# Reordered first attention, q's lower halves on GpSimd, and separate first products in the gated network

## The chip, the cores and the metric

One core of one Trainium2 chip runs the whole kernel. The metric is the device time of one execution in microseconds. Three runs of the kernel before gave 2217.47, 2220.65 and 2222.77 us; the median is 2220.65 us.

## What is computed

The input is 32 samples of 256 tokens, each of width 128, in float32. Two layers follow each other. Each layer is an attention and a feed-forward part, and each part has the form x = x + gate * part(layernorm(x) * (1 + scale) + shift), with gate, scale and shift made per sample from a conditioning vector.

- First attention: RMS norm, then 16 query heads and 8 key and value heads of width 64 (two query heads share one key head). Queries and keys are normalised per head, and the scores go through a soft clamp before the causal softmax:

```
sim = tanh(q @ k.T / 50) * 50 * 64**-0.5
attn = softmax(where(causal, sim, -inf));  out = (attn @ v) @ Wout
```

- First feed-forward part: a router with 16 experts and a shared expert.
- Second attention: 16 heads of width 8 with low-rank projections and rotary parts.
- Second feed-forward part, the gated network, hidden width 512:

```
h = silu((x @ w1) * s1) * ((x @ w2) * s2)
h = gelu((h @ h1) * t1);  h = gelu((h @ h2) * t2);  return (h @ w3) * s3
```

## The kernel before

The kernel keeps all of x in SBUF and runs four stages one after another, each a block with its own instruction list for every engine. The order of the work on each engine is written out by hand: a loop over n, in whose body the pieces of several samples stand in a fixed order, and semaphores join the engines. An engine works its list strictly in order, so a piece that waits holds everything behind it.

**First attention** (function `attention0`, lines 250 to 909). The loop goes over 32 samples. In iteration n the scores of sample n run, while sample n+1 has its queries and keys normalised and turned, sample n+2 is projected, and sample n-1 is gathered and written back to x. The names are:

- The 16 heads are four groups g of four heads. `pe_scores` (L407) writes the scores of a group into the one score buffer `pS` of three PSUM banks; ScalarE's `act_softmax` takes them by tanh (L793) into `th` and by the exponential (L797) into `pr`, one instruction each of 1536 elements per partition. GpSimd's `gp_mask` (L861, two instructions) zeroes the part above the diagonal, and `pe_weighted_values` (L422, L423) multiplies by the values, two heads p at a time. VectorE's `dve_outputs` (L633, L637) divides by the sum, and GpSimd's `gp_sum` (L869) adds the two heads that share a value head into `as`.
- `pe_heads_back` (L444) transposes `as` in two halves t, `act_take_heads` (L803) copies each half into `at`, and `pe_out_project` (L458) multiplies `at` by the output weights. `act_gate` (L787), `pe_out_back` (L464) and `dve_add` (L113) bring it into x.
- Queries and keys are used as a float16 pair, an upper half (the value rounded to float16) and a lower half (what is left). `dve_norm` (L628) scales them, `act_hi` (L775) writes the upper halves and `dve_lo` (L642) the lower ones, by subtraction; u = 0 is k (512 elements), u = 1 is q (1024 elements), and t is the half of the tokens. `pe_turn_k` (L375) and `pe_turn_q` (L391) transpose them into PSUM banks `pW`; `act_take_k` (L781) and `dve_take_q` (L650) copy them out. Two DMAs of SP then make a swapped copy of the keys.
- `pe_project_qk` (L363) makes six products m of 512 columns in the banks `pW`. The products 3 and 4 wait for `dve_take_q` of another sample, product 5 waits for `dve_add`.

In ScalarE's order of iteration n stand tanh and exponential of group 2, then `act_take_heads(n-1, 1)`. On TensorE the matching stretch is: weighted values 3, `pe_out_project(n-1)`, both `pe_turn_k(n+1)`, scores 3, weighted values 4, `pe_turn_q(n+1, 0)`, weighted values 5, `pe_turn_q(n+1, 1)`, `pe_out_back`, products 3, 4 and 5. GpSimd's order is: mask 0, sums 6 and 7 of n-1, mask 1, sums 0 and 1, mask 2, sums 2 and 3, mask 3, sums 4 and 5. Sum 0 of a sample waits until TensorE has transposed the `as` of the sample before, both halves.

**Gated network** (function `mlp`, lines 1718 to 2044). It goes over 16 runs of 512 tokens. All activations are float16 pairs again. For each of four hidden tiles j, `pe_first` (L1783) makes two products, `pA` (for w1) and `pB` (for w2), two matmuls each, and signals once after both. Then `act_tanh` (L1982) reads `pA`, `dve_gated` makes `gf` (L1884) from tanh and `pA` and `uf` (L1888) from `gf` and `pB`, `act_hi` (L1989) and `dve_gated_low` (L1899) split `uf`. `pe_second` and `pe_third` (both L1796) are the two hidden layers in four waves w of 2, 6, 10 and 14 matmuls. Wave w needs the split tile w. `act_gelu` (L2001) takes a finished tile, `dve_parts` (L1878, L1880) splits it. `pe_out` (L1812) is the last product, `act_gate` (L1975) scales it, `pe_back` (L1820) turns it back, and `dve_add` (L1904) adds it to x. `dve_front` (L103), `pe_front` (L1773), `act_modulate` (L1967) and `dve_split_h` (L1878, L1880) prepare the input of a run. The transposes of front and back share one PSUM bank, `pX`; so `pe_back(n-1)` has to wait until `act_modulate(n+1)` has read the bank.

The order on VectorE in iteration n is: low 3 (n), split of the input (n+1), parts 0, 1, 2 of the second layer (n), gated 0 (n+1), parts 3, gated 1, low 0, front (n+2), parts 0 and 1 of the third layer, low 1, parts 2, gated 2, `dve_add(n-1)`, parts 3, low 2, gated 3.

## Time and profile before

| what | value |
|---|---|
| median of three runs | 2220.65 us |
| the profiled execution's own time | 2222.54 us |
| its span | 2220.8 us |
| TensorE busy | 2074.2 us, 93% |
| VectorE busy | 1709.8 us, 77% |
| ScalarE busy | 1444.2 us, 65% |
| GpSimd busy | 521.8 us, 23% |
| mean granted clock of TensorE | 0.978 of full speed |

First attention takes the span from its start to about 1050 us, the gated network from about 1850 us to the end. Busy times are shares of the whole span. Matmuls are pipelined and their recorded ends are modelled, so the start of the next group is a better mark than the end of the last.

### The profile page before, as it was taken

The numbers are of one execution on the slowest core, as the hardware profiler recorded it, in microseconds if no ns is written. First come the engines' busy times: TensorE is split into PE (matmuls) and PEld (weight loads), VectorE is DVE, ScalarE is ACT, GpSimd is POOL, SyncE is SP. The second block draws the span as 40 slices with busy tenths as digits, with TensorE's granted clock in tenths as the row PEclk, the third lists the DMA queues.
The fourth block names the chain that finished last, engine by engine and source line by source line (L and its number), as shares of the span: only waits on it lengthen the run. The fifth ranks groups of instructions, "written<-read, shape, count | busy, mean of one in ns | idle before, by whom it ended". The sixth has DMA issues, their size and how long they took to land. (4 is left out here: it accounts for less than half of the span.)

```text
span 2220.8 us, 40446 instructions
## 1 busy us (share of the span) xinstructions
PE 2074.2 (93%) x14885; PEld 1370.3 (62%) x14885; DVE 1709.8 (77%) x4079; ACT 1444.2 (65%) x1931; POOL 521.8 (23%) x798
## 2 busy tenths in 40 slices
PE   3899999999999999998899999799999996999998
PEld 1577777777777777776444444477777773444443
DVE  3988898888898888983666666577777766888887
ACT  1777777777777777773566666466666663555554
POOL 1243333333333333333000000133333330000000
PEclk9999999999999999997899999899999997999999
DMA  5000000000000000000100000000000000000000
GB/s 160 20 20 20 14 16 21 20 20 20 11 20 20 20 20 20 11 20 20 43 1 1 1 1 0 1 2 2 2 2 2 2 2 1 10 11 15 10 15 19
DMA packets 32836, 35.31 MB, mean 16 GB/s; under 512 B 6865, under 2 KB 26497, under 8 KB 32641
## 3 DMA queue, kind: packets, MB, share of 16 engines
q1 hardware_dynamic: 32640, 32.73, 5.6%
q8 instruction: 120, 1.97, 0.4%
q14 instruction: 76, 0.61, 0.1%
HBM read 11.75 MB, written 4.19 MB: 7 GB/s over the span
## 5 line engine op out<-in xcount | busy, mean ns | idle before, releaser
L861 POOL TENSOR_SCALAR_AFFINE_SELECT pr<-pr 128x512 f32<-128x512 f32 x256 | 208.7, 838 | 534.3 <-ACT pr L797 534.2
L422 PE MATMUL a_pO<-va,pr 128*128 128x66 f32 x2048 | 304.7, 272 | 2.0 <-POOL pr L861 2.0
L422 PEld LDWEIGHTS a_pO<-va,pr 128*128 128x128 f32 x2048 | 273.6, 193 | 19.0 <-issue 14.8
L1620 ACT ACTIVATE c_pr<-c_pS 128x1536 f32<-128x1536 f32 x128 | 186.0, 1453 | 119.2 <-PE c_pS L1432 119.2
L1675 POOL TENSOR_SCALAR_AFFINE_SELECT c_pr<-c_pr 128x512 f32<-128x512 f32 x256 | 158.3, 643 | 265.2 <-DVE c_pr L1540 265.2
L765 ACT ACTIVATE sq<-a_pW 128x512 f32<-128x512 f32 x192 | 114.4, 597 | 143.4 <-PE a_pW L363 140.8
L793 ACT ACTIVATE th<-a_pS 128x1536 f32<-128x1536 f32 x128 | 186.3, 1455 | 30.6 <-PE a_pS L407 30.1
L423 PE MATMUL a_pO<-va,pr 128*128 128x66 f32 x1024 | 199.0, 276 | 0.0
L797 ACT ACTIVATE pr<-th 128x1536 f32<-128x1536 f32 x128 | 189.9, 1484 | 4.1
L407 PE MATMUL a_pS<-qs,k 128*128 128x512 f16 (+1 forms) x1024 | 187.8, 326 | 0.7 <-DVE qs L650 0.7
L1540 DVE TENSOR_SCALAR c_pr<-c_pr 128x1536 f32<-128x1536 f32 x128 | 122.6, 958 | 78.4 <-ACT c_pr L1620 78.4
L869 POOL TENSOR_TENSOR as<-on 128x128 f32<-128x128 f32 x256 | 144.9, 578 | 115.2 <-PE a_pW L444 95.8
L1013 PE MATMUL b_pU<-b_hT,b_uT 128*128 128x512 f32 x320 | 168.9, 611 | 0.0
L1031 PE MATMUL b_pD<-b_a,b_dT 128*128 128x512 f32 x320 | 163.0, 592 | 0.0
L1179 DVE TENSOR_TENSOR b_a<-b_q,b_pC 128x512 f32<-128x512 f32 x128 | 87.7, 685 | 96.3 <-ACT b_q L1263 96.2
L407 PEld LDWEIGHTS a_pS<-qs,k 128*128 128x128 f16 x1024 | 98.9, 98 | 99.8 <-issue 35.3
L1250 ACT ACTIVATE b_r<-b_pU 128x512 f32<-128x512 f32 x160 | 95.4, 596 | 95.6 <-PE b_pU L1013 95.6
L423 PEld LDWEIGHTS a_pO<-va,pr 128*128 128x128 f32 x1024 | 156.4, 193 | 0.0
L581 DVE TENSOR_TENSOR qg<-a_pW,a_gam 128x512 f32<-128x512 f32 x192 | 130.7, 682 | 8.2 <-ACT sq L765 8.1
L633 DVE RECIPROCAL rl<-a_pO 128x4 f32<-128x4 f32 x256 | 44.7, 175 | 112.2 <-PE a_pO L423 112.2
L363 PE MATMUL a_pW<-a_wq,hT 128*128 128x512 f32 x256 | 129.2, 628 | 0.7 <-DVE qs L650 0.7
L1796 PE MATMUL d_pH<-d_a,d_h1T 128*128 128x512 f16 x512 | 122.7, 383 | 3.6 <-DVE d_a L1899 3.6
(259 smaller groups left out, 4439.3 us busy)
## 6 DMA issues: line engine op xcount, KB each, us to landing
k<-k SPq DMA_DIRECT2D x64, 256.0 KB, 3.6
x<-in_L_attn_tokens_dram SPq DMA_DIRECT2D x8, 512.0 KB, 7.0
out_dram<-x SPq DMA_DIRECT2D x16, 256.0 KB, 2.3
d_h<-in_L_ffn_h_w_dram SPq DMA_DIRECT2D x2, 1024.0 KB, 7.3
wmod<-in_L_wmod_dram SPq DMA_DIRECT2D x2, 384.0 KB, 3.6
d_w<-in_L_ffn_w_w_dram SPq DMA_DIRECT2D x3, 256.0 KB, 3.1
a_wq<-in_L_attn_Wq_dram SPq DMA_DIRECT2D x1, 512.0 KB, 6.6
a_wkv<-in_L_attn_Wkv_dram SPq DMA_DIRECT2D x1, 512.0 KB, 6.9
```

The costliest lines, as they stand in the source:

```text
L407: last = pe.matmul(out, kk[:, h // G2, keys * P:(keys + 1) * P], qs[k][:, h:h + G2, keys * P:N], start=first, stop=not first)
L422: pe.matmul(out, w[:, hh * N + t * P:hh * N + (t + 1) * P], v[:, 0, p, :], start=True, stop=t == 0)
L423: last = pe.matmul(out, w[:, HPG * N + hh * P:HPG * N + (hh + 1) * P], v[:, 1, p, :], start=False, stop=True)
L581: dve.tensor_tensor(qg[n % 2][:, t, cols], pW[BANK_OF[m]][:, :], gam[:, cols], ALU.mult).then_inc(s_qg, 1)
L793: act.activation(th[:, :], pS[:, :], ACT.Tanh, scale=1.0 / SOFTCLAMP).then_inc(s_th, 1)
L797: act.activation(pr[g % 2][:, :], th[:, :], ACT.Exp, scale=SOFTCLAMP * DH ** (-0.5)).then_inc(s_pr, 1)
L861: last = gp.affine_select(out=part, in_=part, compare_op=ALU.is_ge, fill=0.0, base=0, pattern=[[0, HPG], [1, P]], channel_multiplier=-1)
L869: gp.tensor_tensor(as_[:, :, p * DH:(p + 1) * DH], o[:, :, 0, :], o[:, :, 1, :], ALU.add).then_inc(s_as, 1)
L1013: pe.matmul(pU[u % 2][:, :], uT[:, t * P:(t + 1) * P], hT[n % 2][:, :], start=True, stop=True).then_inc(s_up, 1)
L1031: pe.matmul(pD[:, :], dT[:, t * D:(t + 1) * D], a[(IT * n + u) % 4][:, :], start=u == 0, stop=u == IT - 1).then_inc(s_dn, 1)
L1620: act.activation(pr[g][:, :, :], pS[:, :, 0:N + P], ACT.Exp, scale=float(1.0 / np.sqrt(np.float32(DQ)))).then_inc(s_ex, 1)
L1675: last = gp.affine_select(out=part, in_=part, compare_op=ALU.is_ge, fill=0.0, base=0, pattern=[[0, HPG], [1, P]], channel_multiplier=-1)
```

## The change

First attention:
- `act_softmax` is split into `act_tanh` and `act_exp`; they follow each other as before, but in group 2 `act_take_heads(n-1, 1)` now stands between them.
- On TensorE `pe_turn_k(n+1, 0)` moves ahead of `pe_out_project(n-1)`, and `pe_turn_q(n+1, 1)` moves ahead of weighted values 5, right behind `pe_turn_q(n+1, 0)`. On VectorE `dve_take_q(n+1, 1)` moves ahead of outputs 5.
- The two lower halves of q (L642, u = 1) leave VectorE for GpSimd, with a semaphore of their own, `s_ql`. On GpSimd the first stands behind sums 0 and 1 and ahead of mask 2, the second behind sum 2 and ahead of sum 3.

Gated network:
- `pe_first` makes one of the two products per call, each with its own signal (`s_in` for `pA`, `s_ib` for `pB`). Tanh and `gf` need only `pA`, `uf` waits for `s_ib`. `gf` has two buffers.
- On TensorE the halves of the first products are spread between waves of the hidden layers, and `pe_front(n+2)` and the output product stand at the end of the iteration, front ahead of first product 3.
- `act_modulate(n+2)` now stands between tanh 3 and the gate at the end of ScalarE's iteration, where `act_modulate(n+1)` stood at the start of it.
- `dve_add(n-1)` moves from behind gated 2 to ahead of gated 0.

```diff
...
         def pe_turn_k(pe, n, t):
-            pe.wait_ge(s_lo, 4 * n + t + 1)
+            pe.wait_ge(s_lo, 2 * n + t + 1)
             if n >= 2:
...
             if j == 0:
-                pe.wait_ge(s_lo, 4 * n + 2 + t + 1)
+                pe.wait_ge(s_ql, 2 * n + t + 1)
...
                     pe_weighted_values(pe, n, 3)
+                if 0 <= n + 1 < B:
+                    pe_turn_k(pe, n + 1, 0)
                 if 0 <= n - 1 < B:
                     pe_out_project(pe, n - 1)
                 if 0 <= n + 1 < B:
-                    pe_turn_k(pe, n + 1, 0)
                     pe_turn_k(pe, n + 1, 1)
                 if 0 <= n < B:
                     pe_scores(pe, n, 3)
                     pe_weighted_values(pe, n, 4)
                 if 0 <= n + 1 < B:
                     pe_turn_q(pe, n + 1, 0)
+                    pe_turn_q(pe, n + 1, 1)
                 if 0 <= n < B:
                     pe_weighted_values(pe, n, 5)
-                if 0 <= n + 1 < B:
-                    pe_turn_q(pe, n + 1, 1)
                 if 0 <= n - 1 < B:
                     pe_out_back(pe, n - 1)
                 if 0 <= n + 2 < B:
...
-                dve.wait_ge(s_lo, 4 * n - 4)
+                dve.wait_ge(s_lo, 2 * n - 2)
+                dve.wait_ge(s_ql, 2 * n - 2)
...
-        def dve_lo(dve, n, u, t):
-            dve.wait_ge(s_hi, 4 * n + 2 * u + t + 1)
+        def lower(eng, n, u, t, done):
+            eng.wait_ge(s_hi, 4 * n + 2 * u + t + 1)
             to, x = ((kp, qg[n % 2][:, t, QW:]), (qp, qg[n % 2][:, t, 0:QW]))[u]
-            dve.tensor_tensor(to[:, t, :, DH:2 * DH], x.rearrange('p (h d) -> p h d', d=DH), to[:, t, :, 0:DH], ALU.subtract).then_inc(s_lo, 1)
+            eng.tensor_tensor(to[:, t, :, DH:2 * DH], x.rearrange('p (h d) -> p h d', d=DH), to[:, t, :, 0:DH], ALU.subtract).then_inc(done, 1)
...
                     dve_sums(dve, n + 2, 0)
-                if 0 <= n + 1 < B:
-                    dve_lo(dve, n + 1, 1, 0)
                 if 0 <= n < B:
                     dve_outputs(dve, n, 2)
                 if 0 <= n + 2 < B:
                     dve_ln(dve, n + 2, 2)
...
-                if 0 <= n + 1 < B:
-                    dve_lo(dve, n + 1, 1, 1)
...
                     dve_take_q(dve, n + 1, 0)
+                    dve_take_q(dve, n + 1, 1)
                 if 0 <= n < B:
                     dve_outputs(dve, n, 5)
-                if 0 <= n + 1 < B:
-                    dve_take_q(dve, n + 1, 1)
                 if 0 <= n + 3 < B:
...
-        def act_softmax(act, n, g):
+        def act_tanh(act, n, g):
             act.wait_ge(s_sc, 4 * n + g + 1)
             if n or g:
                 act.wait_ge(s_pr, 4 * n + g)
             act.activation(th[:, :], pS[:, :], ACT.Tanh, scale=1.0 / SOFTCLAMP).then_inc(s_th, 1)
+
+        def act_exp(act, n, g):
             act.wait_ge(s_th, 4 * n + g + 1)
             if n or g >= 2:
                 act.wait_ge(s_pv, 8 * n + 2 * g - 2)
...
                 if 0 <= n < B:
-                    act_softmax(act, n, 2)
+                    act_tanh(act, n, 2)
                 if 0 <= n - 1 < B:
                     act_take_heads(act, n - 1, 1)
+                if 0 <= n < B:
+                    act_exp(act, n, 2)
                 if 0 <= n + 1 < B:
                     act_hi(act, n + 1, 1, 1)
...
+                if 0 <= n + 1 < B:
+                    lower(gp, n + 1, 1, 0, s_ql)
                 if 0 <= n < B:
                     gp_mask(gp, n, 2)
                     gp_sum(gp, n, 2)
+                if 0 <= n + 1 < B:
+                    lower(gp, n + 1, 1, 1, s_ql)
+                if 0 <= n < B:
                     gp_sum(gp, n, 3)
                 if 0 <= n < B:
                     gp_mask(gp, n, 3)
...
-        def pe_first(pe, n, j):
+        def pe_first(pe, n, j, half):
             if j == 0:
                 pe.wait_ge(s_hx, n + 1)
-            for out, w, taken in ((pA, w1T, s_gf), (pB, w2T, s_uf)):
-                if n or j:
-                    pe.wait_ge(taken, 4 * n + j)
-                for part in range(2):
-                    last = pe.matmul(out[:, :], w[:, j * P:(j + 1) * P], hx[:, part, :], start=part == 0, stop=part == 1)
-            last.then_inc(s_in, 1)
+            out, w, taken, done = ((pA, w1T, s_gf, s_in), (pB, w2T, s_uf, s_ib))[half]
+            if n or j:
+                pe.wait_ge(taken, 4 * n + j)
+            for part in range(2):
+                last = pe.matmul(out[:, :], w[:, j * P:(j + 1) * P], hx[:, part, :], start=part == 0, stop=part == 1)
+            last.then_inc(done, 1)
 
...
-            for n in range(-2, RUNS + 1):
-                if 0 <= n - 1 < RUNS:
-                    for i in range(HT):
-                        pe_out(pe, n - 1, i)
-                if 0 <= n + 1 < RUNS:
-                    pe_front(pe, n + 1)
+            for n in range(-3, RUNS + 1):
...
-                    pe_first(pe, n + 1, 0)
+                    pe_first(pe, n + 1, 0, 0)
                 if 0 <= n < RUNS:
                     pe_third(pe, n, 0)
+                if 0 <= n + 1 < RUNS:
+                    pe_first(pe, n + 1, 0, 1)
+                if 0 <= n < RUNS:
                     pe_third(pe, n, 1)
                 if 0 <= n + 1 < RUNS:
-                    pe_first(pe, n + 1, 1)
+                    pe_first(pe, n + 1, 1, 0)
+                    pe_first(pe, n + 1, 1, 1)
                 if 0 <= n < RUNS:
                     pe_third(pe, n, 2)
                     pe_third(pe, n, 3)
                 if 0 <= n + 1 < RUNS:
-                    pe_first(pe, n + 1, 2)
+                    pe_first(pe, n + 1, 2, 0)
                     pe_second(pe, n + 1, 0)
+                    pe_first(pe, n + 1, 2, 1)
                     pe_second(pe, n + 1, 1)
-                    pe_first(pe, n + 1, 3)
+                if 0 <= n + 2 < RUNS:
+                    pe_front(pe, n + 2)
+                if 0 <= n + 1 < RUNS:
+                    pe_first(pe, n + 1, 3, 0)
+                if 0 <= n < RUNS:
+                    pe_out(pe, n, 0)
+                if 0 <= n + 1 < RUNS:
+                    pe_first(pe, n + 1, 3, 1)
+                if 0 <= n < RUNS:
+                    for i in range(1, HT):
+                        pe_out(pe, n, i)
 
         def dve_front(dve, n):
             if n >= 1:
...
-                dve.wait_ge(s_in, 4 * n)
+                dve.wait_ge(s_ib, 4 * n)
             split(dve, n, hx[:, 0, :], hx[:, 1, :], hf[:, :], s_hh, n + 1, s_hx)
...
-            dve.scalar_tensor_tensor(gf[:, :], th[:, :], 1.0, pA[:, :], ALU.add, ALU.mult).then_inc(s_gf, 1)
+            dve.scalar_tensor_tensor(gf[j % 2][:, :], th[:, :], 1.0, pA[:, :], ALU.add, ALU.mult).then_inc(s_gf, 1)
             dve.wait_ge(s_gf, 4 * n + j + 1)
             if n or j >= 2:
                 dve.wait_ge(s_a1, 4 * n + j - 1)
-            dve.scalar_tensor_tensor(uf[j % 2][:, :], gf[:, :], s12[:, j:j + 1], pB[:, :], ALU.mult, ALU.mult).then_inc(s_uf, 1)
+            dve.wait_ge(s_ib, 4 * n + j + 1)
+            dve.scalar_tensor_tensor(uf[j % 2][:, :], gf[j % 2][:, :], s12[:, j:j + 1], pB[:, :], ALU.mult, ALU.mult).then_inc(s_uf, 1)
 
         def dve_parts(dve, n, layer, o):
...
+                if 0 <= n - 1 < RUNS:
+                    dve_add(dve, n - 1)
                 if 0 <= n + 1 < RUNS:
                     dve_gated(dve, n + 1, 0)
                 if 0 <= n < RUNS:
...
-                if 0 <= n - 1 < RUNS:
-                    dve_add(dve, n - 1)
                 if 0 <= n < RUNS:
                     dve_third(dve, n, 3)
...
                     act_hi(act, n, 3)
-                if 0 <= n + 1 < RUNS:
-                    act_modulate(act, n + 1)
-                if 0 <= n < RUNS:
                     act_second(act, n, 0)
                     act_second(act, n, 1)
                     act_second(act, n, 2)
...
+                if 0 <= n + 2 < RUNS:
+                    act_modulate(act, n + 2)
                 if 0 <= n < RUNS:
                     act_gate(act, n)
 

```

## Rows read from the trace of the kernel before

**Rows 1.** Busy time by stretch: the steady parts of first attention and network

```profile
core 0: us, PE busy (x) PEld busy (x) DVE busy (x) ACT busy (x) POOL busy (x), PEclk, DMA share, GB/s
...
135.00:1000.00 865.00, 833.36 (x6127) 633.28 (x6125) 757.97 (x1632) 663.06 (x766) 314.87 (x458) 1.00 0.07 18
...
1915.00:2200.00 285.00, 271.76 (x1260) 119.20 (x1259) 249.48 (x454) 152.41 (x263) 0.00 (x0) 1.00 0.05 14
```

**Rows 2.** Waits of all engines, 135 to 1000 us: us in total, times, longest

```profile
PE a_pW L458 <- ACT at L803: 28.8, 29, 2.5
```

**Rows 3.** Timeline, one sample of first attention: start, us, engine, line, operation

```profile
421.25 0.87 POOL L869 TENSOR_TENSOR as<-on 128x128 f32<-128x128 f32 x2 [3.11 <-PE a_pW L444]
...
421.30 1.48 ACT L797 ACTIVATE pr<-th 128x1536 f32<-128x1536 f32 x1
...
422.00 0.39 PE L423 MATMUL a_pO<-va,pr 128*128 128x66 f32 x2
...
422.69 0.58 ACT L803 ACTIVATE at<-a_pW 128x512 f32<-128x512 f32 x1
...
423.32 1.99 PE L458 MATMUL a_pW<-at,a_wo 128*128 128x256 f32 x8 [0.94 <-ACT at L803]
...
425.16 1.06 PE L375 MATMUL a_pW<-id,kp 128*128 128x128 f16 x16
...
426.05 1.46 PE L407 MATMUL a_pS<-qs,k 128*128 128x512 f16 x8
...
427.35 0.56 PE L422 MATMUL a_pO<-va,pr 128*128 128x66 f32 x4
...
428.41 0.39 PE L423 MATMUL a_pO<-va,pr 128*128 128x66 f32 x2
...
428.64 0.61 PE L391 MATMUL a_pW<-id,qp 128*128 128x128 f16 x8
```

**Rows 4.** Timeline of first attention: four matmuls and the next group, twice

```profile
409.13 1.94 PE L363 MATMUL a_pW<-a_wq,hT 128*128 128x512 f32 x4
...
410.90 1.46 PE L407 MATMUL a_pS<-qs,k 128*128 128x512 f16 x8
...
431.10 1.95 PE L363 MATMUL a_pW<-a_wq,hT 128*128 128x512 f32 x4
...
433.15 1.12 PE L363 MATMUL a_pW<-a_wkv,hT 128*128 128x512 f32 x2
```

**Rows 5.** Timelines: GpSimd's instructions, one of VectorE beside them

```profile
35.80 2.48 POOL L883 TENSOR_TENSOR a_gam<-a_gam,a_gk 128x512 f32<-128x512 f32 x2
35.88 1.20 DVE L91 TENSOR_TENSOR ln_tmp<-rs 128x4 f32<-128x4 f32 x1
...
431.04 1.23 POOL L861 TENSOR_SCALAR_AFFINE_SELECT pr<-pr 128x512 f32<-128x512 f32 x2 [4.71 <-ACT pr L797]
```

**Rows 6.** Page, part 5: GpSimd's sums

```profile
L869 POOL TENSOR_TENSOR as<-on 128x128 f32<-128x128 f32 x256 | 144.9, 578 | 115.2 <-PE a_pW L444 95.8
```

**Rows 7.** Timeline of the gated network: first tanh, then one run

```profile
1860.95 0.69 ACT L1982 ACTIVATE d_th<-d_pA,d_s1h 128x512 f32<-128x512 f32 x1 [3.17 <-PE d_pB L1783]
...
2051.20 0.43 DVE L1878 CAST d_a<-d_ge 128x512 f16<-128x512 f32 x1 [0.78 <-ACT d_ge L2001]
...
2054.66 0.69 DVE L1884 SCALAR_TENSOR_TENSOR d_gf<-d_th,d_pA 128x512 f32<-128x512 f32 x1 [0.17 <-ACT d_th L1982]
...
2057.55 0.69 DVE L1884 SCALAR_TENSOR_TENSOR d_gf<-d_th,d_pA 128x512 f32<-128x512 f32 x1 [0.36 <-ACT d_th L1982]
...
2070.15 0.69 DVE L1899 TENSOR_TENSOR d_a<-d_uf,d_a 128x512 f16<-128x512 f32 x1 [0.70 <-ACT d_a L1989]
...
2071.17 0.63 PE L1820 MATMUL d_pX<-id,d_og 128*128 128x128 f32 x4 [0.38 <-ACT d_hf L1967]
...
2071.64 3.19 PE L1796 MATMUL d_pH<-d_a,d_h1T 128*128 128x512 f16 x14
...
2072.99 0.43 DVE L1878 CAST d_a<-d_ge 128x512 f16<-128x512 f32 x1 [0.78 <-ACT d_ge L2001]
```

More of the change, by code:

```diff
@@ L289, in attention0 @@
         s_xn, s_xT, s_hT, s_hsq, s_ms, s_msv = (sem(x) for x in ('xn', 'xT', 'hT', 'hsq', 'ms', 'msv'))
-        s_qk, s_sq, s_qg, s_ss, s_f, s_qn, s_hi, s_lo = (
-            sem(x) for x in ('qk', 'sq', 'qg', 'ss', 'f', 'qn', 'hi', 'lo'))
+        s_qk, s_sq, s_qg, s_ss, s_f, s_qn, s_hi, s_lo, s_ql = (
+            sem(x) for x in ('qk', 'sq', 'qg', 'ss', 'f', 'qn', 'hi', 'lo', 'ql'))
         s_qt, s_qs, s_kt, s_ks = (sem(x) for x in ('qt', 'qs', 'kt', 'ks'))
@@ L704, in _ @@
                 if 0 <= n + 1 < B:
-                    dve_lo(dve, n + 1, 0, 0)
+                    lower(dve, n + 1, 0, 0, s_lo)
                 if 0 <= n + 2 < B:
@@ L710, in _ @@
                 if 0 <= n + 1 < B:
-                    dve_lo(dve, n + 1, 0, 1)
+                    lower(dve, n + 1, 0, 1, s_lo)
                 if 0 <= n + 2 < B:
                     dve_sums(dve, n + 2, 0)
-                if 0 <= n + 1 < B:
-                    dve_lo(dve, n + 1, 1, 0)
                 if 0 <= n < B:
@@ L821, in _ @@
                 if 0 <= n < B:
-                    act_softmax(act, n, 0)
+                    act_tanh(act, n, 0)
+                    act_exp(act, n, 0)
                 if 0 <= n + 2 < B:
@@ L826, in _ @@
                 if 0 <= n < B:
-                    act_softmax(act, n, 1)
+                    act_tanh(act, n, 1)
+                    act_exp(act, n, 1)
                 if 0 <= n + 1 < B:
@@ L850, in _ @@
                 if 0 <= n < B:
-                    act_softmax(act, n, 3)
+                    act_tanh(act, n, 3)
+                    act_exp(act, n, 3)
                 if 0 <= n + 2 < B:
@@ L1741, in mlp @@
         hx = sb('hx', [D, 2, W], F16)
-        th, gf, uf = (sb('th', [P, W]), sb('gf', [P, W]), [sb(f'uf{k}', [P, W]) for k in range(2)])
+        th, gf, uf = (sb('th', [P, W]), [sb(f'gf{k}', [P, W]) for k in range(2)], [sb(f'uf{k}', [P, W]) for k in range(2)])
         a1, a2, a3 = (sb(x, [P, HT, 2, W], F16) for x in ('a1', 'a2', 'a3'))
@@ L1754, in mlp @@
         s_xn, s_xT, s_hf, s_hh, s_hx = (sem(x) for x in ('xn', 'xT', 'hf', 'hh', 'hx'))
-        s_in, s_th, s_gf, s_uf, s_uh, s_a1 = (sem(x) for x in ('in', 'th', 'gf', 'uf', 'uh', 'a1'))
+        s_in, s_ib, s_th, s_gf, s_uf, s_uh, s_a1 = (sem(x) for x in ('in', 'ib', 'th', 'gf', 'uf', 'uh', 'a1'))
         s_m2, s_g2, s_h2, s_a2, s_m3, s_g3, s_h3, s_a3 = (sem(x) for x in ('m2', 'g2', 'h2', 'a2', 'm3', 'g3', 'h3', 'a3'))
@@ L1924, in _ @@
             dve.wait_ge(s_c, 1)
-            for n in range(-2, RUNS + 1):
+            for n in range(-3, RUNS + 1):
                 if 0 <= n < RUNS:
@@ L2012, in _ @@
             act.wait_ge(s_c, 1)
-            for n in range(-2, RUNS + 1):
+            for n in range(-3, RUNS + 1):
                 if 0 <= n < RUNS:
                     act_hi(act, n, 3)
-                if 0 <= n + 1 < RUNS:
-                    act_modulate(act, n + 1)
-                if 0 <= n < RUNS:
                     act_second(act, n, 0)
```

## The prediction

> **What bounds the kernel now.** The times by stretch come first, since the change touches two stages with different limits. In the steady part of first attention TensorE is busy 833 of 865 us, VectorE 758, ScalarE 663 and GpSimd 315 [rows 1]; the granted clock is 1.00. TensorE sets the pace there and has 31.6 us of recorded idle time. The waits say what ends it: 28.8 us, 29 times, is TensorE's output projection waiting for ScalarE's copy of the gathered heads [rows 2]. The timeline of one sample shows why: the second half of the heads is summed and turned by 421.25, but ScalarE first works the exponential, 421.30 to 422.78, and copies the heads at 422.69 to 423.27; the projection starts at 423.32 [rows 3]. In the gated network TensorE is busy 271.8 of 285 us and VectorE 249.5 [rows 1], two engines close to each other, so there I look for a loop that goes through both [rows 7].
>
> All sums stand against the profiled execution, 2222.54 us (span 2220.8). The median of the runs is 2220.65, so 1.9 us are taken off at the end.
>
> **First attention, what is removed.** The last matmuls ahead of the projection start at 422.00. A pair like it is followed by the next group 0.23 us later (428.41, 428.64), so TensorE could go on at 422.23; it goes on at 423.32 [rows 3]. That is 1.09 us a sample. The idle row gives 28.8/29 = 0.99, since recorded ends are modelled; I take 1.09. With the copy ahead of the exponential, the heads are ready at 421.30 + 0.58 = 421.88. TensorE first turns half of the keys, half of 426.05 - 425.16 = 0.45 us, and comes to the projection at 422.68: no wait, with 0.80 us to spare. The exponential is 0.58 late, at 423.36; its mask is wanted by weighted values 4 only, see below. The swapped-copy DMAs of SP follow the second key copy on ScalarE, which gets its transposes at about the same time as now, relative to the scores; nothing is added to their queue.
>
> The move of the second transposes of q: products 3 and 4 (four matmuls) are followed by the next group after 1.77 us where nothing waits (409.13 to 410.90) and after 2.05 us where product 5 waits for `dve_add` (431.10 to 433.15) [rows 4]. VectorE's copy of q used to stand between outputs 5 and the normalisation and now stands ahead of both. I take the whole 0.28 us as gained; if outputs 5, which now start later behind weighted values 5, still end last, it is 0.
>
> **First attention, what is added.** The lower halves of q are subtractions of two SBUF inputs of 1024 elements on GpSimd. No such row exists. The nearest are its product of two 512-element inputs, 2.48/2 = 1.24 us [rows 5], and its sums of 128 elements, 0.87/2 = 0.44 us [rows 3]. The slope is 0.80/384 = 2.08 ns an element, so 1024 elements cost 1.24 + 512 x 0.00208 = 2.31 us. From below: the mask, with one input, takes 1.23/2 = 0.62 us for 512 elements [rows 5], so 1.23 us. From above: the sums take 578 ns in the mean of all 256, not 440 [rows 6], because some run beside VectorE; times 1.31 gives 3.03. I take 2.31, the nearest row by kind of instruction. This move has a rule against it: by the Trainium skill (GPSIMD Engine Reference, section 4.1 Engine selection) two-input elementwise work belongs on VectorE, GpSimd being about twice slower, and its section 3.1 has 4497 ns for 2048 elements. Half of that, 2.25 us as an estimate, would give a sum 4 us better than mine; the rows stay with 2.31.
>
> GpSimd has the room (315 of 865 us), but the order counts. The first subtraction could start as soon as its upper half is there, yet it stands behind sums 0 and 1, and these wait for the turned heads: 421.25 to 422.12 [rows 3]. Then in a row: subtraction to 424.43, mask 2 (1.23) to 425.66, sum 2 (0.44) to 426.10, subtraction to 428.41, seen by TensorE at 428.46. TensorE without waits: projection 422.68, plus 1.84 (423.32 to 425.16) keys at 424.52, scores at 424.97, plus 1.30 weighted values 4 at 426.27, plus 1.29 first transposes of q at 427.56, second at 428.01 [rows 3]. So mask 2 comes 0.61 us early, but the second subtraction is 0.45 us late: a new wait of TensorE in each sample, in front of the second transposes of q, with weighted values 5 and all the rest queued behind it. The longer chain is the price of half the gain. It counts twice per sample: each 0.1 us more in one subtraction is 0.2 us of wait.
>
> VectorE loses its two subtractions, which is worth nothing, as TensorE is the limit. It can be held up in turn: an instruction of 4 elements took 1.20 us beside GpSimd's 1.24 [rows 5]. By the Trainium skill (SBUF — State Buffer, section Who interferes with whom) the two engines share a port pair that the first to start holds for its whole instruction; this row agrees. Small steps of the layer norm may now wait up to 2.31 us; one that is held until 424.43 puts the outputs behind it near 425.3, and weighted values 5, which need their buffer, start at 428.46 + 0.45 = 428.9. Free.
>
> Net 1.09 + 0.28 - 0.45 = 0.92 us a sample. Of the 32 samples 31 have both pieces in an iteration: 28.5 us.
>
> **Gated network.** Follow VectorE from parts 0 to the next parts 0: 2051.20 to 2072.99, 21.79 us a run [rows 7]. The loop: VectorE's list up to `uf` 3, ScalarE's upper half, low 3 (2070.15 to 2070.84), TensorE's wave 3 of the second layer, gelu, parts 0. What sits idle in it: 0.17 and 0.36 us before `gf` 0 and `gf` 1, where tanh waits for the `pB` products that it does not read; and wave 3, which could start at 2070.90 and starts at 2071.64, because `pe_back` (2071.17) waits for `act_modulate` to read `pX` [rows 7]. The separate signals let tanh start two matmuls, 0.43 us, earlier, and `dve_add` now stands ahead of gated 0, so VectorE comes there later and finds tanh 0 done; both idles close. The early modulate removes the third, 0.74. Sum 1.27, so 20.52 us a run. Can TensorE follow? Wave 3 has 14 matmuls in 3.19 us, of which the last is 0.38 [rows 7], so 0.216 each; 88 a run make 19.0, and eight transposes (2071.17 to 2071.64 for four) 0.9: 19.9. It can, though the first products 0 and 1 now wait for VectorE, some 0.7 us together. With 14 full intervals between 16 runs: 17.8 us. `pe_front` and the output products keep their cyclic place; their moves cost nothing. In the first run TensorE and ScalarE take turns (tanh 0 idle 3.17 us behind the `pB` products [rows 7]); four tanhs lose a pair of matmuls of 0.4 us each from their chain: 1.5 us, with 0 and 3 as ends.
>
> **Sum:** 28.5 + 17.8 + 1.5 = 47.8; 2222.54 - 47.8 - 1.9 = 2172.8, say **2173 us**. A difference of 0.2% is what a measurement of this kernel can tell from none.
>
> **Rivals.**
> - *The subtractions never bind* (at most 2.08 us each): 1.37 x 31 = 42.5 instead of 28.5, 2159 us. For it: the one-input rate. Against: the two rows with two inputs fit one line. 17%.
> - *They bind harder*, about 2.7 us each, through masks and sums that VectorE holds up: wait 1.23, net 0.14 x 31 = 4; 2197 us. For it: the spread of the sums [rows 6]. Against: VectorE's large two-input instructions in this stretch are just the ones taken away. 13%.
> - *The network gains only its tanh waits*, because VectorE's list, not `pX`, then holds wave 3: 0.53 x 14 = 7.4, 2183 us. VectorE's 249.5 of 285 us speak for it. 14%.
> - *Slower:* GpSimd becomes the limit of first attention in front of the second transposes of q. The point of balance is where 62 x (L - 2.31) = 47.8, so L = 3.08 us a subtraction, just beyond the upper bound; at 3.5 us it gives 2173 + 74 = 2247. By the Trainium skill (SBUF — State Buffer, same section) a subtraction that starts behind a long VectorE instruction would get there. 3%.
> - *The change doesn't do what it says:* the projection waits for something else, for instance the turned heads, and the wait stays: the subtraction's wait is then hidden too, 0.28 x 31 + 19.3 = 28 us, 2193 us. 3%.
>
> My forecast holds 50%, from 2162 to 2186. The range takes in the first three rivals up to the bounds of the subtraction near 2.7 us: 2154 to 2198. Faster 0.95, the same 0.02, slower 0.03: only L of about 3 and more reaches the last two.
>
> **What would show it.** The wait of the output projection for ScalarE is gone, and TensorE waits for GpSimd in front of `pe_turn_q`, 0.3 to 0.6 us a sample; the subtraction's mean is 2.2 to 2.5 us; from scores to scores a sample is 0.9 us shorter. In the network the interval of parts 0 is 20.3 to 20.8 us, `pe_back` no longer waits for modulate, tanh no longer for `pB`. Wrong would be: subtractions over 2.7 us, weighted values 4 waiting for mask 2, or an interval above 21.3 us.

## The result and the profile after

The changed kernel takes 2151.68 us in the median of four runs (2151.37 to 2153.63), the kernel before 2220.73 us (2217.47 to 2222.77): a ratio of 0.9692, 95% interval 0.9675 to 0.9709. The forecast was 2173 us with a range from 2154 to 2198; the time lies 2.3 us below the range. The gain is 69 us where 47.8 were summed. The profiled execution took 2151.95 us, its span is 2150.1 us against 2220.8, so 70.7 us of span are to be placed.

Busy time by stretch, steady parts of both stages (columns as in [rows 1]):

```profile
core 0: us, PE busy (x) PEld busy (x) DVE busy (x) ACT busy (x) POOL busy (x), PEclk, DMA share, GB/s
135.00:960.00 825.00, 824.51 (x6182) 637.97 (x6181) 705.07 (x1572) 664.21 (x770) 401.82 (x514) 1.00 0.08 20
1866.00:2131.00 265.00, 261.17 (x1237) 120.41 (x1236) 243.07 (x450) 148.20 (x258) 0.00 (x0) 1.00 0.05 14
```

In first attention TensorE now has 0.5 us of recorded idle time in 825; before it had 31.6 in 865 [rows 1]. In the network 3.8 us of 265 are left, before 13.2 of 285.

The scores of first attention mark its beginning and end, the first layer's products those of the network. First the lines of these matmuls in the kernel before (count, shortest/median/longest in ns, start of the first and the last):

```profile
L407 PE MATMUL a_pS<-qs,k x1024: 272/330/631, 73.9 to 1027.0; 128*128 128x512 f16 x86, 128*128 128x256 f16 x85
L1783 PEld LDWEIGHTS d_pA<-d_hx,d_w1T x128: 95/98/147, 1859.0 to 2195.4; 128*128 128x128 f16 x128
```

and in the kernel after:

```profile
L407 PE MATMUL a_pS<-qs,k x1024: 271/325/380, 72.2 to 978.4; 128*128 128x512 f16 x86, 128*128 128x256 f16 x85
L1791 PEld LDWEIGHTS d_pA<-d_hx,d_w1T x128: 96/98/118, 1810.3 to 2126.3; 128*128 128x128 f16 x128
```

First attention from first to last scores: 953.1 to 906.2, a gain of 46.9. From there to the network 832.0 and 831.9, no change. Network from first to last product: 336.4 to 316.0, a gain of 20.4. Behind it, to the end of the span, 25.4 to 23.8, 1.6. Ahead of the first scores 1.7. The last is not the change's: the profiled executions below have their first scores between 71.7 and 75.1 us, and the run that has the attention of before begins them at 72.0.

The wait that [rows 2] showed is gone (waits, 135 to 960 us, TensorE and its weight loads):

```profile
PE a_pW L458 <- ACT at L801: 0.5, 1, 0.5
...
PEld a_pW L363 <- DVE x L113: 16.2, 27, 0.6
```

Once, not 29 times, does the projection wait for the heads. A short wait for `dve_add` in front of product 5 is left, 16.2 us in all against 25.4 before. In this stretch no line names GpSimd in front of TensorE's second transposes of q. The timeline of one sample shows that GpSimd has just enough time (this answers to [rows 3] and the first half of [rows 4]):

```profile
405.10 0.87 POOL L872 TENSOR_TENSOR as<-on 128x128 f32<-128x128 f32 x2 [3.09 <-PE a_pW L444]
...
405.92 2.13 POOL L643 TENSOR_TENSOR qp<-qg,qp 128x1024 f16<-128x1024 f32 x1
406.07 0.61 PE L375 MATMUL a_pW<-id,kp 128*128 128x128 f16 x8
...
406.51 1.95 PE L458 MATMUL a_pW<-at,a_wo 128*128 128x256 f32 x8
...
408.01 1.22 POOL L864 TENSOR_SCALAR_AFFINE_SELECT pr<-pr 128x512 f32<-128x512 f32 x2
...
409.20 0.46 POOL L872 TENSOR_TENSOR as<-on 128x128 f32<-128x128 f32 x1
409.61 2.13 POOL L643 TENSOR_TENSOR qp<-qg,qp 128x1024 f16<-128x1024 f32 x1
...
411.33 1.09 PE L391 MATMUL a_pW<-id,qp 128*128 128x128 f16 x16
...
412.25 0.61 PE L422 MATMUL a_pO<-va,pr 128*128 128x66 f32 x4
...
413.82 1.88 PE L363 MATMUL a_pW<-a_wq,hT 128*128 128x512 f32 x4
...
415.54 0.63 PE L363 MATMUL a_pW<-a_wkv,hT 128*128 128x512 f32 x1
```

GpSimd works sums, subtraction, mask, sum, subtraction without a gap from 405.10 to 411.74. TensorE starts the 16 transposes of q at 411.33; the second eight fall due half of their 0.92 us later, at 411.79. The lower half is there 0.05 us before that. The forecast allowed the same 0.05 us from the end of a subtraction to the start of the transposes (428.41 to 428.46), so there is no wait and nothing to spare. The four matmuls of products 3 and 4 are followed after 1.72 us (413.82 to 415.54), before after 2.05. From one sample's L444 to the next, 400.45 to 429.37, are 28.92 us; 46.9 us less for 31 samples are 1.51 us a sample.

The network's VectorE, for the interval of [rows 7]:

```profile
1989.52 0.43 DVE L1896 CAST d_a<-d_ge 128x512 f16<-128x512 f32 x1 [0.47 <-ACT d_ge L2020]
...
2007.79 0.69 DVE L1918 TENSOR_TENSOR d_a<-d_uf,d_a 128x512 f16<-128x512 f32 x1 [0.69 <-ACT d_a L2008]
...
2010.02 0.43 DVE L1896 CAST d_a<-d_ge 128x512 f16<-128x512 f32 x1 [0.47 <-ACT d_ge L2020]
```

Parts 0 to parts 0 is 20.50 us, before 21.79; 20.52 was forecast. `gf` no longer stands in the list of VectorE's waits, and `pe_back` no longer in that of TensorE.

### The profile page after: what moved, and what is told of

The parts are those of the page before. It is cut to its first block and busy times, and to the rows that moved or that the text cites. A ratio compares the mean times of both kernels' runs of the same rounds, so it can differ in the third digit from the quotient of the medians.

```text
span 2150.1 us, 40463 instructions
## 1 busy us (share of the span) xinstructions
PE 2047.2 (95%) x14885; PEld 1372.3 (64%) x14885; DVE 1650.3 (77%) x4015; ACT 1438.3 (67%) x1931; POOL 618.3 (29%) x862
## 3 DMA queue, kind: packets, MB, share of 16 engines
HBM read 11.75 MB, written 4.19 MB: 7 GB/s over the span
## 5 line engine op out<-in xcount | busy, mean ns | idle before, releaser
L864 POOL TENSOR_SCALAR_AFFINE_SELECT pr<-pr 128x512 f32<-128x512 f32 x256 | 202.2, 813 | 370.7 <-ACT pr L795 370.7
L872 POOL TENSOR_TENSOR as<-on 128x128 f32<-128x128 f32 x256 | 116.6, 466 | 109.7 <-PE a_pW L444 95.0
L643 POOL TENSOR_TENSOR qp<-qg,qp 128x1024 f16<-128x1024 f32 x64 | 136.7, 2137 | 25.2 <-ACT qp L771 25.2
```

Source lines behind the costliest of these rows:

```text
L643: eng.tensor_tensor(to[:, t, :, DH:2 * DH], x.rearrange('p (h d) -> p h d', d=DH), to[:, t, :, 0:DH], ALU.subtract).then_inc(done, 1)
L864: last = gp.affine_select(out=part, in_=part, compare_op=ALU.is_ge, fill=0.0, base=0, pattern=[[0, HPG], [1, P]], channel_multiplier=-1)
```

## The experiments

All are the changed kernel with one edit, but for the two that exchange a whole stage. Each ran four times. The kernel before, beside them, took 2218.6 to 2220.0 us in the median, and the ratios given are to it.

**Which stage gained what.** The attention of after with the network of before, and the reverse (function `mlp` exchanged as a whole).

> The gated network is that of the kernel before, first attention that of the kernel after. The two stages touch nothing of each other, so their gains should add. By the two traces the network gave 22 us (20.4 from its first to its last first-layer product, 1.6 behind it): 2151.7 + 22 = 2174 us. If part of that gain came from a different granted clock at the join of the stages, the time would lie elsewhere by more than 3 us.

2174.80 us (2174.40 to 2176.32), ratio 0.9795 (0.9780 to 0.9809): the network's part is worth 23.1 us.

> The first attention of before with the gated network of the change. Theory: the two stages share nothing but the stream x, so the parts add: attention alone gave 2174.8 us, 46 us under before, so this one should take 2151.7 + 46 = 2197.7 us, 2196 to 2200. Rival: the parts do not add (one of them shifts a transfer that the other needs, and the start of the program moves with one of them): outside 2194 to 2202 us. Its scores in first attention should run from first to last in 953 us, as before; whether they begin at 72 or at 74 us shows whether the 1.7 us at the start belong to the change at all.

2196.75 us (2194.08 to 2200.66), ratio 0.9893 (0.9875 to 0.9910). The attention's part is worth 45.1 us; 45.1 and 23.1 make 68.2 of the 69. The parts add, within the noise. The network's products in the two runs, attention only first:

```profile
L1791 PEld LDWEIGHTS d_pA<-d_hx,d_w1T x128: 95/98/151, 1810.5 to 2146.9; 128*128 128x128 f16 x128
```

```profile
L407 PE MATMUL a_pS<-qs,k x1024: 272/324/380, 72.0 to 1025.0; 128*128 128x512 f16 x86, 128*128 128x256 f16 x85
...
L1783 PEld LDWEIGHTS d_pA<-d_hx,d_w1T x128: 95/98/118, 1853.2 to 2169.1; 128*128 128x128 f16 x128
```

336.4 us with the old network, 315.9 with the new one; 953.0 us of scores with the old attention.

**Was it the lower halves' move to GpSimd?** They go back to VectorE, to their old places.

```diff
@@ GpSimd's list
-                    lower(gp, n + 1, 1, 0, s_ql)
...
-                    lower(gp, n + 1, 1, 1, s_ql)
@@ VectorE's list
                     dve_sums(dve, n + 2, 0)
+                    lower(dve, n + 1, 1, 0, s_ql)
                     dve_outputs(dve, n, 2)
...
                     dve_outputs(dve, n, 3)
+                    lower(dve, n + 1, 1, 1, s_ql)
```

> The kernel after with q's two lower halves back on VectorE at their old places. Theory: TensorE is the limit of first attention and VectorE has time, so moving them to GpSimd is worth nothing: 2152 us, within 3. Rival: the relief of VectorE is part of the gain (product 5 waits for its add, which comes earlier on a freer VectorE): 5 us or more above, and TensorE's wait for the add at product 5 is back at 0.2 to 0.3 us a sample.

2152.07 us (2151.29 to 2155.62), ratio 0.9694. The same time as after. The move is worth nothing: relieving VectorE gains nothing, as the prediction said, and the 0.45 us a sample that it charged for GpSimd's side is not there either.

```profile
135.00:960.00 825.00, 824.25 (x6186) 638.12 (x6183) 740.13 (x1631) 664.83 (x770) 312.54 (x457) 1.00 0.08 20
```

VectorE is at 740 us here against 705, GpSimd at 313 against 402, TensorE at 824 in both.

**How near is the wait for GpSimd?** One more sum of 128 elements, about 0.45 us, stands ahead of the second subtraction.

```diff
...
                 if 0 <= n + 1 < B:
+                    gp.wait_ge(s_x, n + 2)
+                    gp.tensor_tensor(extra[:, 2, :], extra[:, 0, :], extra[:, 1, :], ALU.add).then_inc(s_x, 1)
                     lower(gp, n + 1, 1, 1, s_ql)
```

> The kernel after with one more addition of 128 elements (some 0.45 us) on GpSimd ahead of the second subtraction of each sample. Theory: the second subtraction ends just when TensorE wants its transposes, with no slack, so TensorE now waits 0.4 to 0.45 us a sample: 12 to 14 us more, 2164 to 2166 us. Rival: GpSimd's chain has slack of its own and the subtractions never were near the path: 2152 us, no wait of TensorE for GpSimd.

2165.04 us (2163.92 to 2165.16), ratio 0.9748 (0.9732 to 0.9764): 13.4 us more. From first to last scores it is 918.5 us, 12.3 more than after or 0.40 a sample. The added sum is recorded with 0.45 us, but the next instruction starts 0.41 us behind its start:

```profile
416.42 0.45 POOL L909 TENSOR_TENSOR extra<-extra 128x128 f32<-128x128 f32 x1
...
416.83 2.13 POOL L645 TENSOR_TENSOR qp<-qg,qp 128x1024 f16<-128x1024 f32 x1
```

0.41 us more of work gives 0.40 us more of wait, so there was no room that one could measure. The wait of the forecast is there (weight loads, then matmuls):

```profile
PEld a_pW L393 <- POOL qp L645: 12.3, 28, 0.5
...
PE a_pW L393 <- POOL qp L645: 7.5, 28, 0.3
```

Then the same kernel, extra sum included, with the first subtraction ahead of sums 0 and 1, where it does not wait for the turned heads:

```diff
+                if 0 <= n + 1 < B:
+                    lower(gp, n + 1, 1, 0, s_ql)
                 if 0 <= n < B:
                     gp_sum(gp, n, 0)
                     gp_sum(gp, n, 1)
-                if 0 <= n + 1 < B:
-                    lower(gp, n + 1, 1, 0, s_ql)
```

> The kernel with the extra addition on GpSimd (2165.0 us), and the first subtraction moved ahead of sums 0 and 1, so that it no longer waits for TensorE's transposes of the heads. Theory: the wait in front of q's second transposes is the end of a chain that starts with sums 0 and 1; with the first subtraction out of that chain (2.13 us shorter, the extra addition 0.42) there is room again: 2152 us, no wait of TensorE for GpSimd. Rival: the extra work costs by holding VectorE through the shared port, wherever it stands: 2165 us still.

2153.03 us (2152.26 to 2155.90), ratio 0.9703. The extra sum costs nothing measurable now: the scores take 905.8 us (72.9 to 978.7). It is the chain behind the turned heads that has no slack, not GpSimd's total.

**The price that the forecast put in.** Each subtraction of q is made in two instructions of 512 elements.

```diff
...
+            if u:
+                eng.tensor_tensor(to[:, t, 0:half, DH:2 * DH], xv[:, 0:half, :], to[:, t, 0:half, 0:DH], ALU.subtract)
-            eng.tensor_tensor(to[:, t, :, DH:2 * DH], x.rearrange('p (h d) -> p h d', d=DH), to[:, t, :, 0:DH], ALU.subtract).then_inc(done, 1)
+            eng.tensor_tensor(to[:, t, half:, DH:2 * DH], xv[:, half:, :], to[:, t, half:, 0:DH], ALU.subtract).then_inc(done, 1)
```

> The kernel after with each subtraction on GpSimd in two instructions of 512 elements. By 0.45 us for 128 and 2.13 us for 1024 elements an instruction has a fixed part of about 0.2 us, so one subtraction takes about 2.3 us, the price that the prediction used. Theory: TensorE then waits about 0.35 us a sample, as the prediction had it (0.45), 10 us more: 2162 us, between 2158 and 2166. Rival: the wait was misplaced altogether and not mis-sized: 2152 us.

2159.72 us (2158.08 to 2162.28), ratio 0.9727 (0.9712 to 0.9741). The two lines of GpSimd, and the weight loads' wait:

```profile
L645 POOL TENSOR_TENSOR qp<-qg,qp x64: 1146/1157/1447, 61.3 to 964.6; 128x512 f16<-128x512 f32 x64
L646 POOL TENSOR_TENSOR qp<-qg,qp x64: 1148/1158/1611, 62.7 to 965.7; 128x512 f16<-128x512 f32 x64
```

```profile
PEld a_pW L391 <- POOL qp L646: 8.7, 28, 0.3
```

Together 2.31 us, the forecast's very figure, and TensorE waits where the forecast had it. It costs 8.0 us; from first to last scores 915.0 us, 8.8 more or 0.28 a sample, where the forecast worked out 0.45. The starts of GpSimd's instructions give that figure:

```profile
407.96 1.16 POOL L645 TENSOR_TENSOR qp<-qg,qp 128x512 f16<-128x512 f32 x1
409.07 1.16 POOL L646 TENSOR_TENSOR qp<-qg,qp 128x512 f16<-128x512 f32 x1
410.19 1.22 POOL L867 TENSOR_SCALAR_AFFINE_SELECT pr<-pr 128x512 f32<-128x512 f32 x2
```

From the start of a subtraction to the start of the mask are 2.23 us here and 2.09 in the changed kernel (405.92 to 408.01). Twice the difference is 0.28 us, the whole of the wait.

**The heads' copy.** Back behind exponential 2.

```diff
                     act_tanh(act, n, 2)
+                    act_exp(act, n, 2)
                 if 0 <= n - 1 < B:
                     act_take_heads(act, n - 1, 1)
-                if 0 <= n < B:
-                    act_exp(act, n, 2)
```

> The kernel after with the copy of the second half of the heads back behind the exponential of group 2; the first transposes of the keys stay ahead of the projection. Theory: the copy then ends some 0.7 us after TensorE has finished those transposes, so 0.7 us a sample comes back, 31 samples: 22 us, 2174 us, and TensorE's wait for ScalarE at the projection is back at about 0.6 us. Rival: the moved transposes are no cover (they too are held up), the whole 1.09 us come back: 2186 us.

2174.67 us (2173.72 to 2175.81), ratio 0.9798 (0.9783 to 0.9812), 23.0 us more; scores in 927.5 us, 21.3 more or 0.69 a sample. In its timeline of TensorE the half of the keys stands ahead of the wait and covers 0.45 of it:

```profile
415.71 0.61 PE L375 MATMUL a_pW<-id,kp 128*128 128x128 f16 x8
416.82 1.99 PE L458 MATMUL a_pW<-at,a_wo 128*128 128x256 f32 x8 [0.50 <-ACT at L801]
```

Half the keys take 0.45 us, so the projection could start at 415.71 + 0.45 = 416.16. It starts at 416.82, 0.66 us late, next to 1.09 - 0.45 = 0.64 by the forecast's terms.

**The second transposes of q.** Back behind weighted values 5, and their copy behind outputs 5.

```diff
@@ TensorE, and VectorE alike
                     pe_turn_q(pe, n + 1, 0)
-                    pe_turn_q(pe, n + 1, 1)
                     pe_weighted_values(pe, n, 5)
+                    pe_turn_q(pe, n + 1, 1)
```

> The kernel after with the second transposes and the second copy of q back behind weighted values 5 and outputs 5. Theory: product 5 again follows the four matmuls of products 3 and 4 after about 2.05 us instead of 1.72, so 0.3 us a sample: 9 us more, 2161 us. Rival: outputs 5 and the normalisation set the add of VectorE in either order, and the time stays at 2152 us.

2163.51 us (2162.97 to 2166.86), ratio 0.9751 (0.9734 to 0.9769): 11.8 us more; scores in 916.3 us, 10.1 more or 0.33 a sample.

```profile
418.30 1.95 PE L363 MATMUL a_pW<-a_wq,hT 128*128 128x512 f32 x4
420.31 1.13 PE L363 MATMUL a_pW<-a_wkv,hT 128*128 128x512 f32 x2
```

The four matmuls take 2.01 us to the next product again, 0.29 more than after.

**The network's add.** Back behind gated 2.

```diff
-                    dve_add(dve, n - 1)
                     dve_gated(dve, n + 1, 0)
...
                     dve_gated(dve, n + 1, 2)
+                    dve_add(dve, n - 1)
                     dve_third(dve, n, 3)
```

> The kernel after with the network's add into x back behind gated 2. Theory: with the separate signals tanh 0 and tanh 1 are done when VectorE gets there even without the add ahead of them, so the interval of a run stays 20.5 us and only the end of the last run is 0.6 us longer: 2152 to 2153 us. Rival: the add's place is what fills the two idle stretches of 0.17 and 0.36 us (the prediction named both causes together): 0.5 us a run, 7 us, 2159 us.

2167.29 us (2166.74 to 2169.51), ratio 0.9766 (0.9752 to 0.9781): 15.6 us more. Both theories missed. TensorE's waits, 1870 to 2130 us, and its timeline name what both had left out:

```profile
PE d_pX L1781 <- DVE x L1923: 19.0, 12, 1.6
```

```profile
1992.44 0.63 PE L1781 MATMUL d_pX<-id,d_xn 128*128 128x128 f32 x4 [1.58 <-DVE x L1923]
```

`pe_front`, now at the end of an iteration, writes the bank `pX` that the add has to empty first. With the add late it waits 1.58 us, and an interval is 21.67 us (1992.44 to the same mark at 2014.11), 1.17 over the 20.50 of the changed kernel.

**Front and modulate.** Back at the start of an iteration.

```diff
+                if 0 <= n + 1 < RUNS:
+                    pe_front(pe, n + 1)
                     pe_second(pe, n, 2)
...
-                    pe_front(pe, n + 2)
@@ ScalarE
                     act_hi(act, n, 3)
+                    act_modulate(act, n + 1)
                     act_second(act, n, 0)
...
-                    act_modulate(act, n + 2)
```

> The changed kernel, but in the gated network the transposes of the normalised rows (pe_front) and the modulate behind them stand at the start of an iteration again, as before; the early add stays. Theory of the prediction: of the 1.29 us an interval that the network gained, 0.74 us is the wait of pe_back for modulate; it comes back, so 2152 + 14 x 0.74 = 2162 us, and pe_back waits for modulate again. Rival: that wait was covered by other limits and the gain comes from the separate signals and the add: 2152 to 2154 us. Second rival, after the run with the late add (2167, where pe_front waited 1.6 us for the add): the early add in front of gated 0 costs VectorE's list something once nothing needs it there, and the time comes near 2167.

2161.65 us (2159.83 to 2162.33), ratio 0.9732 (0.9718 to 0.9747), 10.0 us more. The time is the theory's and neither rival's; the size of the term can be read more closely. TensorE's `pe_back` and wave 3, here

```profile
2014.73 0.63 PE L1828 MATMUL d_pX<-id,d_og 128*128 128x128 f32 x4
2015.20 3.18 PE L1804 MATMUL d_pH<-d_a,d_h1T 128*128 128x512 f16 x14
```

and in the changed kernel:

```profile
2008.23 0.60 PE L1828 MATMUL d_pX<-id,d_og 128*128 128x128 f32 x4
...
2008.67 3.19 PE L1804 MATMUL d_pH<-d_a,d_h1T 128*128 128x512 f16 x14
```

Low 3, which wave 3 needs, ends at 2013.71 + 0.69 = 2014.40 here and at 2007.79 + 0.69 = 2008.48 there. So wave 3 starts 0.80 us behind it here, as before (2070.84 to 2071.64 [rows 7]), and 0.19 there: 0.61 us, and the interval is 0.62 longer (21.12, low 3 to low 3, 2013.71 to 2034.83).

**Front and add both at their old places.** The edits of the two experiments together.

> The changed kernel with both pe_front with its modulate and the add at their old places; of the network's edits only the separate products with their signals and the cyclic place of the output products are left. Theory: the late add cost 15.6 us by itself only because the early pe_front needs the bank that the add empties. With pe_front late that need is gone, and the time is that of the run with pe_front late alone, near 2162 us. Rival: the add's early place is worth something by itself (it keeps VectorE from coming to gated 0 before tanh 0, and out of the stretch of gated 2 and 3): 2167 us or more, up to the 2174.8 us of the network of before.

2163.09 us (2162.66 to 2163.40), ratio 0.9739 (0.9723 to 0.9755): 1.4 us over the late front alone. So the add's 15.6 us are the price of the early front's bank. Of its own it is worth one thing: behind the last product of the first layer the span goes on for 25.0 us here, 23.8 with the early add.

**Tanh waits for both products.** Only the wait comes back, the products stay apart.

```diff
             act.wait_ge(s_in, 4 * n + j + 1)
+            act.wait_ge(s_ib, 4 * n + j + 1)
```

> The changed kernel, but each tanh of the network waits for both products of the first layer again, though it reads only one. Theory of the prediction: with the add ahead of gated 0 VectorE comes late enough to find tanh 0 done anyway; what comes back is at most the 0.43 us of two matmuls on the intervals where TensorE's products, tanh and the gated step take turns, and the first run's four tanhs (0.4 us each, 1.5): 2153 to 2158 us, 2156 likeliest. Rival: the separate signals are what the network's gain rests on, 0.53 us in each of 14 intervals and more: 2160 us and over.

2164.55 us (2163.37 to 2166.99), ratio 0.9748 (0.9733 to 0.9762): 12.9 us more. The theory missed, the rival holds. ScalarE at the first run, of this kernel:

```profile
1812.42 0.69 ACT L2002 ACTIVATE d_th<-d_pA,d_s1h 128x512 f32<-128x512 f32 x1 [3.23 <-PE d_pB L1791]
1815.86 0.69 ACT L2002 ACTIVATE d_th<-d_pA,d_s1h 128x512 f32<-128x512 f32 x1 [2.75 <-PE d_pB L1791]
...
1824.39 0.69 ACT L2002 ACTIVATE d_th<-d_pA,d_s1h 128x512 f32<-128x512 f32 x1 [0.84 <-PE d_pB L1791]
```

and of the changed kernel:

```profile
1811.34 0.69 ACT L2001 ACTIVATE d_th<-d_pA,d_s1h 128x512 f32<-128x512 f32 x1 [2.32 <-PE d_pA L1791]
1813.87 0.69 ACT L2001 ACTIVATE d_th<-d_pA,d_s1h 128x512 f32<-128x512 f32 x1 [1.85 <-PE d_pA L1791]
...
1821.11 0.69 ACT L2001 ACTIVATE d_th<-d_pA,d_s1h 128x512 f32<-128x512 f32 x1 [0.77 <-PE d_pA L1791]
```

The fourth tanh comes 3.3 us later (3.1 without the 0.17 us by which its stage begins later), the second falls behind by 0.9 us more than the first: `pB` 1 has to wait for `uf` 0, which is a gated step behind, and tanh 1 waited for `pB` 1. In the steady runs the same chain holds:

```profile
2003.21 0.61 PE L1791 MATMUL d_pB<-d_hx,d_w2T 128*128 128x512 f16 x2 [0.18 <-DVE d_uf L1907]
...
2003.90 0.69 ACT L2002 ACTIVATE d_th<-d_pA,d_s1h 128x512 f32<-128x512 f32 x1 [1.67 <-PE d_pB L1791]
...
2004.62 0.69 DVE L1902 SCALAR_TENSOR_TENSOR d_gf<-d_th,d_pA 128x512 f32<-128x512 f32 x1 [0.41 <-ACT d_th L2002]
```

VectorE waits 0.41 us before `gf` 1 and is late with everything behind; the interval is 21.05 us (low 3, 1995.63 to 2016.68), 0.55 longer. 15 x 0.55 and 3.1 make 11.4 of the 12.9.

## Why the prediction was wrong

The step that failed is a term of the sum: the wait for GpSimd's subtraction, put at 0.45 us a sample, 14.0 us in all, was none. Place and mechanism were right, the size was not. With that term at nothing the sum gives 2159 us, which lies inside the range; what took the time below the range are several smaller terms that all erred to the same side. Term by term:

- **The heads' copy: right.** 1.09 us a sample, no wait at the projection, 0.45 us of cover by the keys. The late copy gave 0.66 us of lateness where the terms say 0.64.
- **Product 5: right, a little small.** 0.33 us (2.05 to 1.72) instead of 0.28; undone, 0.29 in the timeline and 0.33 a sample between the scores.
- **The price of the subtraction on GpSimd: the step that failed.** "The slope is 0.80/384 = 2.08 ns an element, so 1024 elements cost 1.24 + 512 x 0.00208 = 2.31 us" was taken over into a wait of 0.45 us a sample, 14 us in all. The page has 2137 ns in the mean of 64:

```profile
L643 POOL TENSOR_TENSOR qp<-qg,qp 128x1024 f16<-128x1024 f32 x64 | 136.7, 2137 | 25.2 <-ACT qp L771 25.2
```

  It counts twice, as the prediction says, so 2 x 0.18 = 0.36 us of the 0.45 are gone with that. The rest is that durations were added where starts count. Sums, subtraction, mask and sum start 0.82, 2.09, 1.19 and 0.41 us apart (405.10, 405.92, 408.01, 409.20, 409.61), and the forecast's figures for them, with the measured 2.13 for the subtraction, were 0.87, 2.13, 1.23 and 0.44: 0.16 us too much. Against this TensorE comes 0.07 us earlier than worked out (411.79 - 405.10 = 6.69 us behind the first sum, not 428.01 - 421.25 = 6.76). So 0.45 - 0.36 - 0.16 + 0.07 = 0. The run with 2.31 us shows the second part alone: 0.28 us of wait and not 0.45. By the same terms it would be 0.45 - 0.16 + 0.07 = 0.36, less 2 x 0.04 because each subtraction there has one start more that overlaps.

  The slope's upper point, 1.24 us, was an instruction of another kind: an f32 product, at the start of the kernel. A subtraction of 512 elements with an f16 input and an f16 result takes 1.157, which gives 0.98/512 = 1.91 ns an element instead of 2.08. Whether the types or the operation make that difference was not tested. The case measured is the prediction's first rival (17%), "at most 2.08 us each". Its bound was drawn too low for the same reason: at the measured 2.13 the wait is just gone.
- **The figure of the Trainium skill.** By the Trainium skill (GPSIMD Engine Reference, section 3.1) half of 4497 ns, 2.25 us as an estimate, was too long as well, though nearer; the measured 2.13 decides. The Trainium skill's rule that such work belongs on VectorE (same page, section 4.1) agrees with these rows for the instruction, 1.215 us there against 2.133, and it makes no difference to this kernel's time: 2151.68 us with the subtractions on GpSimd, 2152.07 on VectorE.
- **The network's interval: right to 0.02 us** (20.50 against 20.52), **but its working was not.** What the early modulate gives was put at 0.74 and is 0.61: the forecast let wave 3 start 0.06 us behind low 3, but `pe_back`'s own transposes stand ahead of it, and it starts 0.19 behind. The tanh waits were put at 0.17 + 0.36, and 1.29 - 0.61 = 0.68 is left for them; 0.55 of it come back with the wait for both products, the other 0.13 stay open. The prediction held that the add ahead of gated 0 would help close them; the run with add and front late shows no part of that, it is the signal that does. Two errors cancelled, so the agreement to 0.02 us is luck. That the early front needs the early add stood nowhere in it.
- **First run and end of the network: too small.** 1.5 us for four tanhs of a matmul pair each. Shown are 0.85 us at tanh 0 (4.19 us behind modulate before, 3.34 after) and 1.70 from tanh 0 to tanh 3 (11.47 and 9.77 us), and 1.2 us behind the last first-layer product, by the early add. The network came to 23.1 us in the medians against 19.3.
- **What the forecast lacks, in all.** 22.9 us between the spans: 14.0 for the wait on GpSimd, 4.4 for product 5 and for small overlaps that were not taken apart (46.9/31 = 1.51 us a sample against 1.37), 2.7 for the network's ends and 1.7 for the start, which differs from execution to execution. They sum to 22.8; the last 0.1 lies between the two stages.
- **The rivals.** *Bind harder* and *slower* fell with the price: 2.13 us in the median and 2.42 in the longest of all 64, never 2.7. *Only the tanh waits* fell: an interval of 20.50. *Doesn't do what it says* fell with the wait of the projection.

## What to carry to other kernels

A chain whose end is worth 0.45 us of wait per round hangs on prices to 0.1 us: for the price of an operation that the trace does not show take a row of the same kind, types included, and add up the distances between starts and not the durations. If the chain counts a doubtful price twice, its error is the forecast's. And when a writer of a shared bank is moved ahead, ask who empties the bank: the add moved by itself looked like nothing and was worth 15.6 us.

## What was not expected of the hardware

A very short step of VectorE can wait out a GpSimd instruction that is already running. The scaling of two elements (`ss<-ag`) in the kernel before, after, and with the lower halves back on VectorE:

```profile
L549 DVE TENSOR_SCALAR ss<-ag x30: 158/637/640, 51.0 to 910.7; 128x2 f32<-128x2 f32 x30
```

```profile
L549 DVE TENSOR_SCALAR ss<-ag x30: 158/1669/1679, 48.7 to 869.0; 128x2 f32<-128x2 f32 x30
```

```profile
L549 DVE TENSOR_SCALAR ss<-ag x30: 158/160/640, 50.6 to 869.2; 128x2 f32<-128x2 f32 x30
```

It takes 158 ns at the least. Before the change it takes 637 in the median: in one sample it starts at 423.70 and ends at 424.34, as two masks (422.86 to 424.32) end. Beside the subtractions it takes 1669: in the sample above it starts at 406.41 under the subtraction of 405.92 and ends at 408.08, as that ends at 408.05. A subtraction of the keys, 684 ns in the median, is held too: one starts at 86.56, behind the start of GpSimd's subtraction (86.41 to 88.55), and takes 2531. That a short step is held was known [rows 5]; that it ends with the other's instruction at two very different lengths is what these lines add, and the Trainium skill (SBUF — State Buffer, section Who interferes with whom) has such a hold last for the whole instruction. Here it was free: VectorE has 120 us of 825 to spare.

It goes the other way too. Where VectorE's product of 1536 elements (L629) runs from 399.18 to 400.93 us, GpSimd's two masks, which take 1.22 us elsewhere, take 2.71 from 399.29. In the sample above neither subtraction of q stands beside such a product; what 2.13 us would become there was not tested.
